# The routing of a mixture-of-experts stage: fewer steps on VectorE, dense tile one-hots, and a share of the lane one-hots on GpSimd

## The reference

```
x = x + 0.5 * ffn(layernorm(x))
x = x + attn(layernorm(x))
x = x + 0.5 * ffn(layernorm(x))

ffn(x):   scores = x @ gate_w.T + gate_b + bias             # 8 experts
          top_scores, top_idx = top_k(scores, 2); gates = softmax(top_scores)
          comb[t, e] = the gate of token t for expert e, 0 if it wasn't chosen
          y_e = w2_e(silu(w1_e(x) + b1_e)) + b2_e           # 512 -> 352 -> 512
          out[t] = sum over e of comb[t, e] * y_e[t]
```

## Time and profile before

| | |
|---|---|
| median of three runs | 840.39 us (839.42 to 841.66) |
| the profiled execution: its own time | 840.20 us |
| its span, first to last instruction | 838.5 us |
| PE busy | 766.4 us (91%) |
| DVE busy | 608.8 us (73%) |
| ACT busy | 360.9 us (43%) |
| POOL busy | 231.4 us (28%) |
| mean granted TensorE clock | 0.961 of full speed |

### The profile page before, as it was taken

How to read it: one execution, slowest core, us unless ns; L and a number is a source line. 1 busy time by engine, 2 the same in 40 slices (tenths; PEclk the granted TensorE clock), 3 DMA queues, 4 the chain that set the end, 5 groups by cost and what they waited for, 6 DMA issues and landing times.

```text
span 838.5 us, 14108 instructions
## 1 busy us (share of the span) xinstructions
PE 766.4 (91%) x4218; PEld 423.2 (50%) x4219; DVE 608.8 (73%) x1024; ACT 360.9 (43%) x626; POOL 231.4 (28%) x225
## 2 busy tenths in 40 slices
PE   8689899999997997998999999999925999999998
PEld 5345465656563444444444444445503566666663
DVE  6884756666656669999989998896876555555557
ACT  5855333444433437446534654443251333333331
POOL 3212644444532001101210211102102444444431
PEclk9899999999998998899999999999966999999999
DMA  9973648985743701610451110266463573333698
GB/s 315 402 285 136 223 149 314 335 297 163 241 160 106 182 1 51 106 46 1 83 94 26 53 24 14 63 229 148 173 253 115 183 268 120 113 116 121 223 313 305
DMA packets 44955, 137.27 MB, mean 164 GB/s; under 512 B 5488, under 2 KB 5488, under 8 KB 41584
## 3 DMA queue, kind: packets, MB, share of 16 engines
q1 hardware_dynamic: 27536, 86.38, 28.6%
q0 software_dynamic: 17376, 50.34, 21.7%
HBM read 85.32 MB, written 51.38 MB: 163 GB/s over the span
## 4 chain that ended last, share of the span: by engine, by line
PE 74%; DVE 14%; DMA 4%; ACT 3%; issue 3%; POOL 2%; SPq 0%; DVEq 0%; ACTq 0%; POOLq 0%
PE bank L653 61%; PE bank L647 5%; PE bank L746 3%; DMA space<-xn_rows,slot_src 3%; PE bank L916 2%; PE bank L832 1%; DVE space L1406 1%; DVE space L1466 1%; DVE space L1685 1%; POOL space L574 1%; DVE space L1682 1%; DMA space<-x_in 1%; DVE bst L1397 1%; PE bank L850 1%; POOL rstd L606 1%
## 5 line engine op out<-in xcount | busy, mean ns | idle before, releaser
L653 PE MATMUL bank<-space 128*128 (+3 forms) x2958 | 580.2, 349 | 22.5 <-DVE space L1470 12.8
L653 PEld LDWEIGHTS bank<-space 128*128 128x128 f16 (+1 forms) x2958 | 276.3, 99 | 270.9 <-issue 25.2
L578 POOL DMA_INDIRECT y_rows<-space,slot_dst x78 | 86.4, 1108 | 157.1 <-DVE space L1538 156.5
L574 POOL DMA_INDIRECT space<-xn_rows,slot_src x78 | 81.9, 1050 | 124.2 <-PE bank L647 65.2
L1094 ACT ACTIVATE space<-bank 128x512 f16<-128x512 f32 x78 | 46.5, 597 | 146.4 <-PE bank L647 138.1
L1538 DVE TENSOR_SCALAR space<-bank,slot_gate 128x512 f32<-128x512 f32 x78 | 58.5, 751 | 60.1 <-PE bank L653 59.2
L1525 DVE SCALAR_TENSOR_TENSOR space<-bank,space 128x352 f32<-128x352 f32 x78 | 40.9, 524 | 60.7 <-PE bank L653 46.8
L1104 ACT ACTIVATE space<-bank 128x384 f16<-128x384 f32 x78 | 38.3, 490 | 94.6 <-PE bank L746 94.6
L647 PE MATMUL bank<-ident,space 128*128 128x128 f32 x440 | 66.3, 281 | 13.3 <-DMA space<-xn_rows,slot_src 11.4
L1519 DVE TENSOR_TENSOR space<-bank,space 128x512 f16<-128x512 f32 x78 | 53.9, 691 | 33.4 <-ACT space L1094 31.0
L1682 DVE SCALAR_TENSOR_TENSOR space<-space,cang 128x512 f32<-128x512 f32 x84 | 63.0, 751 | 5.4 <-ACT space L1186 3.2
(11 more groups left out here) (199 smaller groups left out, 749.5 us busy)
## 6 DMA issues: line engine op xcount, KB each, us to landing
space<-ffn_w SPq DMA_DIRECT2D x8, 1472.0 KB, 11.2
w_saved<-space SPq DMA_DIRECT2D x8, 1472.0 KB
space<-w_saved SPq DMA_DIRECT2D x8, 1472.0 KB, 8.9
xn_rows<-space SPq DMA_DIRECT2D x8, 1024.0 KB, 7.2
space<-y_rows SPq DMA_DIRECT2D x16, 512.0 KB, 6.6
space<-x_in SPq DMA_DIRECT2D x7, 1024.0 KB, 6.8
space<-att_w SPq DMA_DIRECT2D x12, 518.0 KB
space<-y_rows POOLq DMA_DIRECT2D x6, 1024.0 KB, 9.2
```

The costliest lines, as they stand in the source:

```text
L574: gp.indirect_dma_start(dst, None, rows, bass.IndirectOffsetOnAxis(ap=index, axis=0)).then_inc(done, 16)
L578: gp.indirect_dma_start(y_rows, bass.IndirectOffsetOnAxis(ap=slot_dst[:, t:t + 1], axis=0), yo[:, t % 2], None).then_inc(y_st[t % 2], 16)
L653: last = pe.matmul(dst, a, b, start=(n == 0), stop=(n == len(terms) - 1))
```

## The change

- `M8` is written as expert by tile, and a scan over tiles (`SC`, restarted at each expert) is taken of it before PE sees it. PE now makes the count from the scanned mask first (one product with ones), and then the rank in two products into one bank: ones times the scan, plus `others` times the mask. The copy, the scan and the subtraction that DVE did on the counts are gone, and so is an addition (`EX` plus base).
- The second maximum is masked in one instruction instead of two.
- The two masks lie side by side (`OH12`), so that slots are picked by one multiplication and one sum of 256 elements rather than two of each with 128.
- `OHhi`, `OHtok` and `OHgate` are stored with the token tile innermost. They are made from `hi16` and a table `tiles16` (each slot tile's number, 16 times), which POOL writes. PE reads them with a step of 16 elements.
- POOL makes the lane one-hot of the last eight token tiles of the second choice, with eight instructions, after DVE has written the lanes in fp32 (`k1`, `s_lo16`); PE waits for them by `s_olo`.
- PE's 32 matmuls can start at the first choice (`s_ohs` counts both choices).
- The counts that are needed for `ready` are copied from PSUM (`SCL`).

```
+SHARED = 8
...
-            OHhi.append(at([2, NT, HI_PAD], F16))
-        OHtok = [lay2([2, NT, HI_PAD], F16)]
+            OHhi.append(at([2, HI_PAD, NT], F16))
+        OHtok = [lay2([2, HI_PAD, NT], F16)]
...
-        OHgate = [lay([2, 2 * NT, HI_PAD], F16)]
+        OHgate = [lay([2, 2, HI_PAD, NT], F16)]
...
-        S, S2, OH1, OH2, KEY, M8, QP = (lay([NT, E]) for _ in range(7))
-        raws_first = Layout(lay.at - 6 * NT * E)([PAIR], rows=E)
-        CE, SC, EX = (lay([E, NT]) for _ in range(3))
...
+        S, S2, KEY, QP = (lay([NT, E]) for _ in range(4))
+        raws_first = Layout(lay.at - 3 * NT * E)([PAIR], rows=E)
+        OH12, QOH = (lay([2, NT, E]) for _ in range(2))
+        OH1, OH2 = OH12[:, 0], OH12[:, 1]
+        M8, SC = (lay([E, NT]) for _ in range(2))
+        SCL = lay([2, NT])
...
+        tiles16 = [Layout((E - 1) * FW)([HI_PAD, NT], F16), Layout(35400)([HI_PAD, NT], F16)]
...
-            select(before[:, :], ones[:, :], ALU.is_gt, 0.0, 0, [[1, P]], -1)
+            seq(gp.memset(others[:, :], 0.0))
+            select(others[:, :], others[:, :], ALU.is_gt, -1.0, 0, [[1, P]], -1)
...
+            def tile_numbers(ph):
+                count(tiles16[ph], 0, [[1, HI_PAD], [0, NT]], 0).then_inc(s_tiles, 1)
+
+            def lanes_shared(ph):
+                gp.wait_ge(s_lo16, ph + 1)
+                for t in range(NT - SHARED, NT):
+                    last = gp.tensor_scalar(OHlo[ph][:, 1, t], lane16[:, :], k1[:, t:t + 1], None, ALU.is_equal)
+                last.then_inc(s_olo, 1)
...
             more_constants()
+            tile_numbers(0)
+            lanes_shared(0)
             slots(0)
...
+            gp.wait_ge(c_out, NT)
+            tile_numbers(1)
+            lanes_shared(1)
             slots(1)
...
             def route(ph):
                 pe.wait_ge(s_onehot, ph + 1)
-                chosen = M8.rearrange("p a b -> p (a b)")
-                products(bank[3][:, 0:NT * E], [(before[:, :], chosen)])
-                products(bank[4][:, 0:NT * E], [(ones[:, :], chosen)]).then_inc(s_count, 1)
+                chosen, summed = (x.rearrange("p a b -> p (a b)") for x in (M8, SC))
+                products(bank[4][:, 0:NT * E], [(ones[:, :], summed)]).then_inc(s_count, 1)
+                products(bank[3][:, 0:NT * E], [(ones[:, :], summed), (others[:, :], chosen)]).then_inc(s_rank, 1)
                 if not ph:
                     pe.wait_ge(consts, 3)
                     for n in range(2 * len(CUTS) - 1):
                         low_piece(OWN + n // len(CUTS), n % len(CUTS))
-                pe.wait_ge(s_ohs, ph + 1)
-                products(bank[5][:, 0:SLOT_TILES],
-                         [(OHlo[ph][:, k, t, :], OHtok[ph][:, k, t, 0:SLOT_TILES]) for k in (0, 1) for t in range(NT)]).then_inc(s_inv, 1)
+                for k in (0, 1):
+                    pe.wait_ge(s_ohs, 2 * ph + k + 1)
+                    for t in range(NT):
+                        if k and t == NT - SHARED:
+                            pe.wait_ge(s_olo, ph + 1)
+                        last = pe.matmul(bank[5][:, 0:SLOT_TILES], OHlo[ph][:, k, t, :], OHtok[ph][:, k, 0:SLOT_TILES, t],
+                                         start=k + t == 0, stop=k == 1 and t == NT - 1)
+                last.then_inc(s_inv, 1)
 
             def slot_gates(ph):
                 pe.wait_ge(s_gates, ph + 1)
                 products(bank[5][:, KH * P:KH * P + SLOT_TILES],
-                         [(OHlo[ph][:, k, t, :], OHgate[ph][:, k, half * NT + t, 0:SLOT_TILES])
+                         [(OHlo[ph][:, k, t, :], OHgate[ph][:, k, half, 0:SLOT_TILES, t])
                           for k in (0, 1) for half in (0, 1) for t in range(NT)]).then_inc(s_slotg, 1)
...
-                seq(v.scalar_tensor_tensor(S2.rearrange(flat), OH1.rearrange(flat), 0.0, S.rearrange(flat), ALU.is_equal, ALU.mult))
-                seq(v.scalar_tensor_tensor(S2.rearrange(flat), OH1.rearrange(flat), -3.0e38, S2.rearrange(flat), ALU.mult, ALU.add))
+                seq(v.scalar_tensor_tensor(S2.rearrange(flat), OH1.rearrange(flat), -3.0e38, S.rearrange(flat), ALU.mult, ALU.add))
...
-                v.tensor_tensor(M8, OH1, OH2, ALU.add).then_inc(s_onehot, 1)
+                seq(v.tensor_tensor(M8.rearrange("p e t -> p t e"), OH1, OH2, ALU.add))
+                v.tensor_tensor_scan(SC.rearrange(flat), restart[:, :, :].rearrange(flat), M8.rearrange(flat), 0.0,
+                                     ALU.mult, ALU.add).then_inc(s_onehot, 1)
...
                 v.wait_ge(s_count, ph + 1)
-                seq(v.tensor_copy(CE, bank[4][:, 0:NT * E].rearrange("p (t e) -> p e t", e=E)))
-                seq(v.tensor_tensor_scan(SC.rearrange(flat), restart[:, :, :].rearrange(flat), CE.rearrange(flat), 0.0, ALU.mult, ALU.add))
-                ch(v.tensor_tensor(EX, SC, CE, ALU.subtract))
-
-                seq(v.tensor_scalar(tl, SC[:, :, NT - 1], 1.0, float(P - 1), ALU.max, ALU.add))
+                counts = bank[4][:, 0:NT * E].rearrange("p (e t) -> p e t", e=E)
+                seq(v.tensor_scalar(tl, counts[:, :, NT - 1], 1.0, float(P - 1), ALU.max, ALU.add))
...
-                seq(v.tensor_tensor(EX, EX, eb(base8), ALU.add))
-                seq(v.tensor_tensor(QP, bank[3][:, 0:NT * E].rearrange("p (a b) -> p a b", b=E),
-                                    EX.rearrange("p e t -> p t e"), ALU.add))
-                for k, oh_ in ((0, OH1), (1, OH2)):
-                    seq(v.tensor_tensor(KEY, QP, oh_, ALU.mult))
-                    seq(v.reduce_sum(posf[:, k], KEY, AX))
+                v.wait_ge(s_rank, ph + 1)
+                seq(v.tensor_tensor(QP, bank[3][:, 0:NT * E].rearrange("p (e t) -> p t e", e=E),
+                                    base8.unsqueeze(1).to_broadcast([P, NT, E]), ALU.add))
+                seq(v.tensor_tensor(QOH, QP.unsqueeze(1).to_broadcast([P, 2, NT, E]), OH12, ALU.mult))
+                seq(v.reduce_sum(posf, QOH, AX))
                 round_down(hi_f, posf, lo_f)
                 ch(v.tensor_copy(hi16, hi_f))
                 seq(v.scalar_tensor_tensor(lo16, hi_f, -float(P), posf, ALU.mult, ALU.add))
+                v.scalar_tensor_tensor(k1, hi_f[:, 1], -float(P), posf[:, 1], ALU.mult, ALU.add).then_inc(s_lo16, 1)
+                v.wait_ge(s_tiles, ph + 1)
                 for k in (0, 1):
-                    ch(v.tensor_tensor(OHlo[ph][:, k], lo16[:, k].unsqueeze(2).to_broadcast([P, NT, P]),
-                                       lane16[:, :].unsqueeze(1).to_broadcast([P, NT, P]), ALU.is_equal))
-                    seq(v.tensor_tensor(OHhi[ph][:, k, :, 0:SLOT_TILES], hi16[:, k].unsqueeze(2).to_broadcast([P, NT, SLOT_TILES]),
-                                        lane16[:, 0:SLOT_TILES].unsqueeze(1).to_broadcast([P, NT, SLOT_TILES]), ALU.is_equal))
-                    last = v.tensor_tensor(OHtok[ph][:, k, :, 0:SLOT_TILES], OHhi[ph][:, k, :, 0:SLOT_TILES],
-                                           toks[:, k].unsqueeze(2).to_broadcast([P, NT, SLOT_TILES]), ALU.mult)
-                    if k == 0:
-                        ch(last)
-                last.then_inc(s_ohs, 1)
-
+                    own = NT - SHARED * k
+                    ch(v.tensor_tensor(OHlo[ph][:, k, 0:own], lo16[:, k, 0:own].unsqueeze(2).to_broadcast([P, own, P]),
+                                       lane16[:, :].unsqueeze(1).to_broadcast([P, own, P]), ALU.is_equal))
+                    seq(v.tensor_tensor(OHhi[ph][:, k, 0:SLOT_TILES], hi16[:, k].unsqueeze(1).to_broadcast([P, SLOT_TILES, NT]),
+                                        tiles16[ph][:, 0:SLOT_TILES], ALU.is_equal))
+                    last = v.tensor_tensor(OHtok[ph][:, k, 0:SLOT_TILES], OHhi[ph][:, k, 0:SLOT_TILES],
+                                           toks[:, k].unsqueeze(1).to_broadcast([P, SLOT_TILES, NT]), ALU.mult)
+                    last.then_inc(s_ohs, 1)
+
+                ch(v.tensor_copy(SCL, counts[:, E - 2:E]))
...
-                        last = v.tensor_tensor(OHgate[ph][:, k, half * NT:(half + 1) * NT, 0:SLOT_TILES], OHhi[ph][:, k, :, 0:SLOT_TILES],
-                                               gpart[:, half, k].unsqueeze(2).to_broadcast([P, NT, SLOT_TILES]), ALU.mult)
+                        last = v.tensor_tensor(OHgate[ph][:, k, half, 0:SLOT_TILES], OHhi[ph][:, k, 0:SLOT_TILES],
+                                               gpart[:, half, k].unsqueeze(1).to_broadcast([P, SLOT_TILES, NT]), ALU.mult)
...
-                seq(v.tensor_scalar(posf, SC[:, E - 2:E], 63.5, 1.0 / P, ALU.add, ALU.mult))
+                seq(v.tensor_scalar(posf, SCL, 63.5, 1.0 / P, ALU.add, ALU.mult))
```

More of the change, by code:

```diff
@@ L119, in build @@
         ones = sb("ones", [P, P])
-        before = sb("before", [P, P])
+        others = sb("others", [P, P])
         headmean = sb("headmean", [P, P])
@@ L242, in build @@
         rows_last = [lg[1][:, g] for g in range(NCH - 1)] + [x2_tail]
-        OHtok.append(lay([2, NT, HI_PAD], F16))
```

(10 more changed lines are left out.)

## The result

The changed kernel takes 847.37 us (median of 4 runs, 845.89 to 851.38) where the kernel before takes 840.66 in the same series (4 runs, 839.42 to 841.66): a ratio of 1.009, 95% interval 1.0068 to 1.0112. The forecast was 837.4, so both the sign and the size were wrong.

A forecast was written before the change was run, and what follows sets the result against it. DVE was taken to bound phase 1 routing, PE's weight pieces phase 0. From 840.20 us, -3.4 (L1481 with the port) - 0.25 (tail) + 0.5 (strided columns) + 0.3 (phase 0) = -2.85 gave 837.4; range 835.6 to 839.8.

The forecast's parts named there:

- Steps 1 to 6: Phase 1 routing on DVE and PE: fewer mask, scan and pick instructions; first `OHlo` starts 1.92 us earlier.
- step 1: Phase 1: one masking instruction less, -0.33 us; strided mask write 0 to 0.08, taken as 0; PE starts 0.13 later.
- Steps 7 and 8: Phase 1 one-hots on DVE: second `OHlo` 1024 elements fewer, -1.07 us; `OHhi` and `OHtok` at 0.48 each, -1.3.
- Rival D: Dense one-hots on DVE are no faster: +1.3 us, tail saves nothing, +0.25; 838.95 us, chance 0.1.
- The port: Phase 1: POOL's eight instructions and DVE make each other wait; +0.9 us on DVE's path, bounds 0 and +2.6.
- Step 9: Phase 1: PE has 16 matmuls left instead of 32, is no longer last; L1481 4.3 us earlier with DVE undisturbed.
- rival E: GpSimd's lanes come last, PE waits: 840.8 us at 0.63 a strip, chance 0.08; 843.8 at 1.01; slower case 0.05.
- Step 10: End of `route`: four instructions of L1499 save 1.3 us of 2.97; `x_low` starts when ACT is done, -0.25.
- Step 11: PE reads one-hots with a step of 32 bytes: 176 matmuls cost between 0 and 1.1 us, taken +0.5.
- Rival C: Strided columns cost PE half its rate: +1.1 us instead of 0.5; 838.0 us, chance 0.12.
- Phase 0: One more product ahead of PE's pieces and a later mask: +0.3 us, between 0 and 0.6; DVE's savings hidden.
- What follows moves with it: After the routing, clock and weight transfers are released by events that move with it, so it shifts as a whole.

The follow-up runs named there:

- e2: Changed kernel with VectorE making all lane one-hots, no strips on GpSimd; 844.05 us, ratio 1.0057 to the kernel before.
- e7: Changed kernel with tile one-hots stored in groups of four token tiles and four GpSimd strips instead of eight; 837.61 us, ratio 0.9982 to the kernel before.
- e11: Changed kernel with groups of four token tiles, seven of phase 0's eleven pieces before the 32 matmuls, no strips; 835.49 us, ratio 0.9959 to the kernel before.
- e5: Changed kernel with columns side by side, no strips, and 96 matmuls probing six column steps ahead of the gate matmuls; 846.59 us, one run.

## Why the prediction was wrong, point by point

- **Steps 1 to 6** (masks and scans, 1.92 earlier): right, 1.89. The masked write with a step costs 0.38 instead of 0.29 (L1466), the most that step 1 allowed. The rank products were in time: L1481 follows without a wait.
- **Steps 7 and 8** (fewer lanes, dense one-hots): right. 1.22 for the second choice, 0.48 for a product. Rival D is out.
- **The port** (+0.9, DVE's path): too dear. The last one-hot came 4.1 earlier where the sum without the port said 4.29. Only the later products stretched, by some 0.1 each (0.57 and 0.55 for 0.47). It was POOL that waited: its first strip took 2.89 us and ended 0.41 behind DVE's first L1494, the second 1.64 and ended 0.38 behind the second L1492. That all eight would exclude DVE for their whole length, +2.6, was not seen either.
- **Step 9** (PE has 16 matmuls left and is not last): wrong, and the second step that failed. It is rival E's mechanism, which had a chance of 0.13, though not E's price. A strip alone costs 0.58 us, but six of the eight ran from 630.37 on, when DVE was nearly done. PE had the last of them 2.83 us after DVE's last one-hot. L1506 came 1.85 earlier, not 3.4. E's own formula put the last lane 5.28 + 8d behind the start of `OHlo`; it came at 8.18, a d of 0.36 where E began at 0.63. By that formula L1506 would still have come 2.2 earlier; the last eight matmuls, strided, at 0.75 us for the 0.3 that E had for them, account for the rest.
- **Step 10** (the tail): right in kind. `x_low` now waits 1.56 us for ACT, so DVE's tail is off the path. It starts 1.85 after the first transposes instead of 2.03, 0.18 for the forecast 0.25.
- **Step 11** (strided columns, +0.5 of at most 1.1): **this is the step that failed.** Measured: 32 matmuls from 0.97 to 2.51 and 64 from 1.95 to 4.85 in phase 0, and about as much in phase 1, some 9 us of PE's time. In the table of stretches 1.5 + 2.2 + 2.2 us of it show, and the 12 matmuls behind the gates add 1.5 for the clock in phase 0 (their 1.1 in phase 1 goes under in the wait that before has there). The sum had 0.5 for the columns, with 1.1 as the most, and nothing for the clock. The error was the upper bound. "Half rate" stood in no row; it was the smallest penalty that I could name, used as the largest. A column costs 4.3 times as much, not twice. Rival C named the right mechanism with that same wrong factor, and the Trainium skill's note on cachelines (SBUF — State Buffer, Door 1: The DMA port swizzle) gave no factor to put there. An honest bound would have asked for the dearest access in the trace, or left the top open and made the range wider upward.
- **Phase 0** (+0.3): the second product moved the first piece 0.43 later, and most was lost in the slow first pieces: the 32 matmuls came 0.12 later, behind 0.21 of masks. Right. But "PE is full there" was read only as cover for DVE; it also means that each us added to PE's own matmuls is a us of the kernel.
- **What follows moves with it**: right for the attention stage (-0.2), wrong for the clock behind the gates.

The sum again with measured terms, on the profiled execution: 0.97 to the first product, +3.5 for the rest of phase 0, -0.2 in attention, -1.52 to the gather in phase 1 and +2.85 behind it: 5.6. Of this, 0.76 lies ahead of anything that the change touches but start-up, and no run tells whether it is the change's. The gain that was forecast was made on DVE, 4.1 us in each phase. In phase 0 it was hidden by the pieces as forecast, in phase 1 POOL and the first strided matmuls took 2.3 of it, and the strided gates the rest.

## What to carry to other kernels

A layout has a writer and readers: price the reader on the engine that bounds the kernel, from a row with the same step, and where there is none, measure a ladder of steps first; one run did it here. A layout between both extremes (pairs of the inner index) gave both engines their fast rate. Where two engines make each other wait, work handed to the idle one should be counted as starting when its neighbour is done (six of eight strips here), and a faster producer is worth only what the order of the consumer's queue lets it be.

## What the runs showed of the hardware

- TensorE's moving columns in fp16, 39 of them: 0.025 us at a step of 2 or 4 bytes, 0.038 at 8, 0.073 at 16 and 32, 0.069 at 64, all at a granted clock of 1.00. At 0.50 it was 0.033 side by side and 0.074 at 32 bytes.
- The granted clock fell to 0.50 behind gate matmuls at 0.076 with PE recorded as busy throughout (both phases of the changed kernel and of e2), and did not behind those at 0.041 or less in e7 to e11. Behind e5's 48 matmuls at 0.069 to 0.073 it fell in phase 0 and not in phase 1.
- VectorE, a product of two fp16 inputs with 624 elements: 0.48 us when runs of two or more lie side by side, 1.27 when one input is read with a step of 32 bytes, 3.0 when the output is written with a step of 80.
- GpSimd's strip of 128 fp16 elements: 0.58 us alone, 2.89 and 1.64 beside VectorE's large instructions, which themselves lost about 0.1.
